# A Mamba mixer between two feed-forward blocks: the skip product and the last states of a block change engines

## The reference

```python
x_in = inp - mean(inp)
x, z = split(x_in @ W_in)                  # 512 -> 2 x 1024
x = silu(depthwise_conv(x, conv_w, 4 taps) + conv_b)
Bm, Cm = split(x @ W_x)                    # 16 states each
delta = softplus(x @ W_dt + b_dt)
for t:  h = exp(delta_t * A) * h + delta_t * B_t * x_t      # 1024 x 16 states
        y_t = sum over the states of h * C_t
y = (y + x * D) * silu(z)
out = y @ W_out + residual
```

## Time and profile before

| | |
|---|---|
| time, median of 3 | 5427.12 us (5426.79 to 5429.24) |
| the profiled execution's own time | 5428.6 us |
| its span in the profile | 5426.0 us |
| mean granted TensorE clock | 0.993 |
| busy: TensorE, VectorE, GpSimd, ScalarE | 97%, 89%, 76%, 67% |

### The profile page before, as it was taken

The page is one execution under the profiler, slowest core; times in us unless marked ns, Lnnn a source line. Parts: engine busy times, 40 slices in busy tenths (PEclk is TensorE's granted clock), DMA queues, the critical chain, the costliest instruction groups (busy, mean ns, idle before and its releaser), DMA issues. The chain is left out here.

```text
span 5426.0 us, 78894 instructions
## 1 busy us (share of the span) xinstructions
PE 5245.9 (97%) x22912; PEld 4241.1 (78%) x22912; DVE 4827.3 (89%) x8114; ACT 3653.4 (67%) x9184; POOL 4105.3 (76%) x2212
## 2 busy tenths in 40 slices
PE   8999989999999999999999999999999999979999
PEld 6777778787787787778777887787787878758887
DVE  6777679999999999999999999999999999976775
ACT  4565567777777777777777777777777777744443
POOL 1111079999999999999999999999999999941110
PEclk9999999999999999999999999999999999989999
DMA  2222221111111111111111111111111111111111
GB/s 80 93 70 93 97 90 38 49 56 58 48 44 44 44 44 44 44 44 44 48 44 44 44 45 47 54 59 53 44 44 44 44 44 44 44 62 62 55 53 47
DMA packets 137340, 291.34 MB, mean 54 GB/s; under 512 B 23280, under 2 KB 40688, under 8 KB 136944
## 3 DMA queue, kind: packets, MB, share of 16 engines
q1 hardware_dynamic: 136944, 286.75, 16.0%
HBM read 218.53 MB, written 68.18 MB: 53 GB/s over the span
## 5 line engine op out<-in xcount | busy, mean ns | idle before, releaser
L962 POOL TENSOR_TENSOR mx_dbu<-mx_bs,mx_du 128x1024 f32<-128x1024 f32 x1024 | 2404.9, 2358 | 32.9 <-POOL mx_du L955 18.8
L1098 ACT ACTIVATE mx_ps_da<-mx_dl,mx_a 128x256 f32<-128x256 f32 x4096 | 1776.4, 465 | 71.3 <-DVE mx_hp L1181 36.8
L1181 DVE TENSOR_TENSOR_SCAN mx_hp<-mx_ps_da,mx_hst,mx_dbu 128x256 f32<-128x256 f32 x2048 | 1505.0, 735 | 92.7 <-ACT mx_ps_da L1098 92.7
L1181 DVE TENSOR_TENSOR_SCAN mx_ps_da<-mx_ps_da,mx_hst,mx_dbu 128x256 f32<-128x256 f32 x2048 | 1416.6, 737 | 17.9 <-ACT mx_hst L1030 7.5
L943 POOL TENSOR_TENSOR mx_hp<-mx_hp,mx_cs 128x1024 f32<-128x1024 f32 (+1 forms) x576 | 1219.5, 2117 | 5.5 <-ACT mx_hst L1030 5.5
L1342 PE MATMUL mx_ps_y<-mx_hc,mx_ident 128*128 128x256 f32 x4096 | 1052.7, 380 | 0.0
L1352 PE MATMUL mx_ps_y<-mx_hp,mx_ident 128*128 128x256 f32 x3584 | 947.3, 381 | 15.1 <-POOL mx_hp L943 15.1
L1307 PE MATMUL mx_ps_m<-mx_u,mx_w_dt 128*128 128x256 f32 x4096 | 926.1, 379 | 2.8 <-issue 2.5
L1307 PEld LDWEIGHTS mx_ps_m<-mx_u,mx_w_dt 128*128 128x128 f32 x4096 | 779.1, 190 | 108.3 <-issue 2.9
L1342 PEld LDWEIGHTS mx_ps_y<-mx_hc,mx_ident 128*128 128x128 f32 x4096 | 780.0, 190 | 105.5
L1352 PEld LDWEIGHTS mx_ps_y<-mx_hp,mx_ident 128*128 128x128 f32 x3584 | 678.5, 190 | 182.3 <-issue 73.2
(11 more groups left out here) (117 smaller groups left out, 6905.9 us busy)
## 6 DMA issues: line engine op xcount, KB each, us to landing
mx_bs<-bc_scratch SPq DMA_DIRECT2D x128, 512.0 KB, 3.9
mx_cs<-bc_scratch SPq DMA_DIRECT2D x128, 512.0 KB, 4.0
mx_hT<-hT_scratch SPq DMA_DIRECT2D x32, 518.0 KB, 4.3
hT_scratch<-f_h2T SPq DMA_DIRECT2D x16, 1024.0 KB, 8.5
mx_xo<-xs_scratch SPq DMA_DIRECT2D x32, 512.0 KB, 5.0
x_scratch<-mx_xo SPq DMA_DIRECT2D x32, 512.0 KB, 5.6
f_x<-in_L_attn_inp SPq DMA_DIRECT2D x12, 1024.0 KB, 6.3
xs_scratch<-f_x SPq DMA_DIRECT2D x12, 1024.0 KB, 4.3
```

The source lines that it names most:

```text
L962: G.tensor_tensor(dbu[:, n % NM], bs[:, g], bcast(du[:, b % 2, :], SG), ALU.mult).then_inc(s_m1, 1)
L1098: ins = A.activation(ps_da[DA_BANK[p]][:, k, :], dl[:, b % NL, :], ACT.Exp, scale=a_sb[:, b, s:s + 1])
L1181: ins = V.tensor_tensor_scan(da if half == 0 else hp[:, n % NH, k, :], da, dbu[:, n % NM, s, :], hst[:, b, SG * g + s:SG * g + s + 1], ALU ...
```

## The change

ScalarE writes u x D into the block's bank before TensorE's first matmul of the block, in a new function `skip`, and all of TensorE's matmuls accumulate (start=False). `skip` stands at the last unit of the block's own number (4b + 3), between the unit's two pairs of decays; it waits for u and for `gated` of the block before last. TensorE's first matmul waits for `skip`. On VectorE `with_skip` is gone. `sum_states` leaves out one state in each of the last two units of a block, and VectorE adds both in `add_last_states`, one after the other, with a wait after each. The wait of `first_tap` for the reader of u two chunks back is now for GpSimd's product delta x u.

```diff
+        SKIP_AT = [NG * b + NG - 1 for b in range(ND)]
+        def y_sum(b):
+            return ps_y[b % 2][:, 0:T]
@@ ScalarE, first_tap
-                    act.wait_ge(s_yd, ND * (c - 2) + (b + 1))
+                    act.wait_ge(s_du, ND * (c - 2) + (b + 1))
@@ ScalarE
+            def skip(c, cp, b):
+                act.wait_ge(s_u, ND * c + 2 * (b // 2) + 2)
+                if not (is0(c) and b < 2):
+                    act.wait_ge(s_g, ND * c + (b - 1))
+                A.activation(y_sum(b), u[:, cp, b, :], ACT.Copy, scale=d_sb[:, b:b + 1]).then_inc(s_yd, 1)
@@ ScalarE, body, after first_tap and before the second pair of decays
+                            for bb, s in due(SKIP_AT, n, i):
+                                skip(i + s, (par + s) % 2, bb)
@@ VectorE
-            def with_skip(c, cp, b):
-                dve.wait_ge(s_r, NU * c + NG * (b + 1))
-                V.scalar_tensor_tensor(out=ps_y[b % 2][:, 0:T], in0=u[:, cp, b, :], scalar=d_sb[:, b:b + 1],
-                                       in1=ps_y[b % 2][:, 0:T], op0=ALU.mult, op1=ALU.add).then_inc(s_yd, 1)
-            def add_last_state(c, b):
-                y = ps_y[b % 2][:, 0:T]
-                dve.wait_ge(s_yd, ND * c + (b + 1))
-                V.tensor_tensor(y, y, hp[:, (NG * (b + 1) - 1) % NH, SG - SD - 1, :], ALU.add).then_inc(s_ya, 1)
+            def add_last_states(c, b):
+                y = y_sum(b)
+                dve.wait_ge(s_r, NU * c + NG * (b + 1))
+                for n in (NG * b + NG - 2, NG * b + NG - 1):
+                    V.tensor_tensor(y, y, hp[:, n % NH, SG - SD - 1, :], ALU.add).then_inc(s_ya, 1)
+                    dve.wait_ge(s_ya, 2 * (ND * c + b) + n % 2 + 1)
@@ VectorE, gated
-                dve.wait_ge(s_ya, ND * c + (b + 1))
@@ VectorE, body
-                    for b, s in due(YG_AT, n, i):
-                        with_skip(i + s, (par + s) % 2, b)
@@ TensorE, sum_psum_states
-                if g == 0 and (b >= 2 or not is0(c)):
-                    pe.wait_ge(s_g, ND * c + (b - 1))
+                if g == 0:
+                    pe.wait_ge(s_yd, ND * c + (b + 1))
-                                   start=(g == 0 and k == 0), stop=False, skip_group_check=True)
+                                   start=False, stop=False, skip_group_check=True)
@@ TensorE, sum_states
-                last = 1 if g == NG - 1 else 0
+                last = 1 if g >= NG - 2 else 0
```

More of the change, by code:

```diff
@@ L759, in mixer_phase @@
         s_zs = sem("z_silu")
-        s_yd = sem("yd_ready")
-        s_ya = sem("last_state_added")
+        s_yd = sem("skip_in_psum")
+        s_ya = sem("last_states_added")
         s_g = sem("gated")
@@ L1164, in gated @@
                 dve.wait_ge(s_zs, ND * c + (b + 1))
-                dve.wait_ge(s_ya, ND * c + (b + 1))
-                V.tensor_tensor(q, ps_y[b % 2][:, 0:T], q, ALU.mult).then_inc(s_g, 1)
+                V.tensor_tensor(q, y_sum(b), q, ALU.mult).then_inc(s_g, 1)
             def residual(c, j):
@@ L1214, in finish @@
                 for b, s in due(YG_AT, n, i):
-                    add_last_state(i + s, b)
+                    add_last_states(i + s, b)
                 for j, s in due(EVAC_AT, n, i):
@@ L1253, in epilogue @@
                     for b in due_after(YG_AT, n):
-                        with_skip(LAST, LAST % 2, b)
-                        add_last_state(LAST, b)
+                        add_last_states(LAST, b)
                         gated(LAST, LAST % 2, b)
@@ L1337, in sum_psum_states @@
                 b, g = divmod(n, NG)
-                if g == 0 and (b >= 2 or not is0(c)):
-                    pe.wait_ge(s_g, ND * c + (b - 1))
+                if g == 0:
+                    pe.wait_ge(s_yd, ND * c + (b + 1))
                 pe.wait_ge(s_m2, NU * c + (n + 1))
                 for k in range(SD):
-                    ins = M.matmul(ps_y[b % 2][:, 0:T], ident[:, :], hc[:, n % NC, k, :],
-                                   start=(g == 0 and k == 0), stop=False, skip_group_check=True)
+                    ins = M.matmul(y_sum(b), ident[:, :], hc[:, n % NC, k, :],
+                                   start=False, stop=False, skip_group_check=True)
                 ins.then_inc(s_rc, 1)
@@ L1349, in sum_states @@
                 pe.wait_ge(s_pr, NU * c + (n + 1))
-                last = 1 if g == NG - 1 else 0
+                last = 1 if g >= NG - 2 else 0
                 for k in range(SG - SD - last):
-                    ins = M.matmul(ps_y[b % 2][:, 0:T], ident[:, :], hp[:, n % NH, k, :],
+                    ins = M.matmul(y_sum(b), ident[:, :], hp[:, n % NH, k, :],
                                    start=False, stop=(g == NG - 1), skip_group_check=True)
```

## The result

The changed kernel takes 5356.47 us (median of 4 runs, 5354.89 to 5357.36) against 5426.95: ratio 0.9869, 95% interval 0.9852 to 0.9886. That is 70.5 us less, inside the range that was given, where 58 were forecast.

The account below looks back on a forecast made before the run. A loop of TensorE (pace in five blocks of eight) and VectorE (three) bounds the kernel. 2.0 us less a chunk over 30 chunks: 5428.6 - 60 + 1.5 = 5370, as median 5369; range 5345 to 5422.

Parts of the forecast that it names:

- TensorE's part: One matmul fewer per block, between gate product and next input product: 0.43 us a block, 3.44 a chunk, leaving 121.33.
- The loop: TensorE and VectorE hold each other block by block; convolution may lag 1.25 us; chunk 127.42 us before, 125.41 after.
- VectorE's part: Two dependent adds at 0.51 us replace skip and add: +0.12 in seven blocks, +0.32 in one, 124.80 a chunk.
- The rule cited from the Trainium skill: Every VectorE operation pays its flush, semaphores cost nothing extra, so the swap saves; as a rival 5344 us, chance 0.05.
- ScalarE's part: Eight added activations a chunk, 0.43 us each, 3.4 in all, behind the fourth unit's first decay pair, absorbed by waiting time.
- 4.6 us early, at least 0.8: At a block's first state on TensorE: ScalarE's activation done 4.6 us early, still 0.8 where the convolution lags by 3.8.
- a sign of being wrong: At TensorE's first matmul of a block: the prediction is wrong if TensorE waits for the new activation; no size given.
- The ends: In half of the first chunk and in the last, VectorE leads throughout and each block costs 0.12 more: +1.5 us.

Follow-up runs that it names:

- all three: Kernel before, but VectorE adds two states and keeps the skip product; ScalarE and the overwriting first matmul stay as before: 5450.30 us, ratio 1.0036.
- no adds: Changed kernel, skip still with ScalarE, but TensorE sums all the states and VectorE adds none: 5458.01 us, ratio 1.0052.
- one add: Changed kernel, skip still with ScalarE, but VectorE adds one state and TensorE sums the rest: 5404.42 us, ratio 0.9956.
- the moved wait: Kernel before, with VectorE's wait for its add moved to right after the add, ahead of the wait for silu(z): 5418.08 us, ratio 0.9976.
- the second order of waits: Changed kernel, with the wait after VectorE's second add moved behind the output sum, after the wait for silu(z): 5352.12 us, then 5355.31 us when repeated.

## Why the prediction was right, point by point

**TensorE's part** was right to the digit: 0.43 us off each block, 16.41 and 14.69. That the gain hangs on it was shown by putting the matmul back (5422.6).

**The loop** was right in form. It gave 127.42 and 125.41 us a chunk; the chunks that are not at the turn of a batch row are 127.5 in most cases before, and 125.1 to 126.0 now. It gave 4.08 us of waiting for TensorE, and the chunk from 1982.39 to 2107.82, 125.43 us for 121.33 of work, has 4.1. Of the experiments, 127.5 to 128 was expected for "all three" (127.2 to 127.7 where the clock held), 127.4 for the matmul put back (127.5), 128.2 for no adds (128.9) and 126.5 for one add (127.0). In the last two it is 0.5 to 0.7 too low, because the loop has two engines and there ScalarE's decays hold VectorE by 0.31 and 0.67 us.

**VectorE's part** held the term that was mis-sized. I took 0.51 us for each of the two adds; they take 0.47 and 0.44 (0.91 up to the gating product), so a free block did not grow by 0.12 but stayed at 15.36. In the block with an output sum the growth was 0.37 (1.07 for 0.70), not 0.32. With 15.36 and 0.37 the same loop gives 125.0; with the block of the other output sum at the 16.07 us read (2176.52 to 2192.59), where that reckoning has 15.74, it gives 125.2. That is 2.2 us off a chunk, for the 2.3 read and the 2.0 forecast, and the difference over 30 chunks is 7 to 8 us of the missing 12. The rule cited from the Trainium skill, "VectorE: DVE Perf Modes", on the DRAIN you can't avoid, that a semaphore after each operation costs nothing extra, came nearer to the sum than my 0.51, but by accident: dependence does cost (0.31 free, 0.44 dependent), and the moved wait shows that part of my 0.51 was not dependence at all.

**ScalarE's part** was right: 0.46 us per activation (forecast 0.43), nothing of it paid. But "4.6 us early, at least 0.8" for TensorE's new wait was wrong: TensorE waits 0.28 us for it in one block of a chunk, since there the convolution lags most and TensorE is furthest ahead, while the activation comes late, behind a table load (it starts at 2091.07). The prediction named such a wait as a sign of being wrong. It costs nothing all the same, because the next gate product would have waited that much longer; and, which no step of mine had, it keeps the clock up. That the time came out as near to the forecast as it did is in part luck: without any wait at that point the kernel takes 5384 us.

**The ends**: I expected +1.5 us there and found -2.7, which is another 4 of the missing 12; and the -2.7 are not the change's doing, so this part of the gain is chance. They are there in full at the input product behind the mixer's first B/C product (699.18 for 701.88), before anything that the change touches has run: that B/C product takes 3.64 us for 4.71, at a granted clock of 1.00 for 0.76 (694.74 to 701.80 in the kernel before), and the gate product before that starts 1.06 us earlier. Later in the run-up the kernel before also takes 3.45 us for the gate product at 737.41 after a wait of 4.30, and the changed one 2.00 at 734.71 after 2.28, with 1.75 us of wait for the skip at 726.11; by the second B/C product nothing of that is left.

## What to carry to other kernels

Where three engines are within 2% of each other, write down for each block who leads and how much lag the coupling allows: the gain of an edit is read from that chain, and here 3.44 us of saved work became 2.3. Here work was worth moving off one leading engine only where the other leading engine did not pay for it; a third one with idle time in the right place made the trade pay, and it became the next limit itself 0.4 us further on. And when TensorE begins to wait, look at where its waits lie and at its granted clock, not only at their sum.

## What I had not expected of the hardware

A single TensorE wait of 2.10 us was in some chunks followed by a granted clock of 0.57 for 3.3 us, some 1.7 us lost, and in others by 1.00; split into 0.48 and 1.36 us that end 8 us apart, it cost nothing in any chunk between turns, and the 28 us came back. And a VectorE step that reads the result of the step before it starts 0.44 us after that one's start or 0.51, and moving the wait between them turned the one into the other; since the second order of waits also gave 0.44 in the changed kernel, which detail decides is open.
